# One fused attention and FFN kernel on one core: the sums move to VectorE, the job clusters are regrouped

## The reference, cut to what matters

```python
lat, ctx = layernorm(layernorm(x)), layernorm(context)
q, k, v = lat @ Wq, ctx @ Wk, ctx @ Wv                   # 16 heads of 64
attn = softmax(clip(q @ k.T * 64 ** -0.5, -11, 11))
x = x + tanh(g_xattn) * ((attn @ v) @ Wo + bo)
# FFN: weights rounded in blocks of 32 (lpbq_dequant), activations to 16 bits (act_qdq)
h = act_qdq(layernorm(x))
up, gate = act_qdq(h @ Wup.T), act_qdq(h @ Wgate.T)
gate = act_qdq(gate * fixed_qdq_u16(sigmoid(gate)))
x = x + tanh(g_ffn) * (act_qdq(gate * up) @ Wdown.T)
```

## Time and profile before

| | |
|---|---|
| median of 3 runs | 1286.16 us (1285.85 to 1286.87) |
| the profiled execution | 1289.14 us, span of its instructions 1287.2 us |
| PE busy | 1137.3 us |
| DVE busy | 1114.6 us |
| ACT busy | 599.4 us |
| POOL busy | 735.1 us |
| mean granted clock of TensorE | 0.962 of 2.4 GHz |

### The profile page before, as it was taken

One profiled execution on the slowest core, in us unless ns is written; L12 is line 12 of the kernel. 1 busy time (PEld: TensorE's weight loads), 2 busy tenths in 40 slices (PEclk: granted clock), 3 DMA queues, 4 the chain that ended last, 5 costly groups with the idle time before them and its releaser, 6 DMA issues.

```text
span 1287.2 us, 21518 instructions
## 1 busy us (share of the span) xinstructions
PE 1137.3 (88%) x8427; PEld 497.1 (39%) x8427; DVE 1114.6 (87%) x1435; ACT 599.4 (47%) x682; POOL 735.1 (57%) x457
## 2 busy tenths in 40 slices
PE   4999999999999999999999999998789987699028
PEld 2443333333333333333333333333223332487028
DVE  7588988898889888988898889899899999848986
ACT  2454444444444444444444444443345443249542
POOL 1596666666666666666666666667676565102400
PEclk9999999999999999999999999999899999699559
DMA  4000000000000000000000020000000000000002
GB/s 153 1 2 13 6 1 1 17 2 1 1 18 1 1 1 17 1 1 1 18 1 1 1 69 23 2 1 1 1 1 1 2 1 1 1 1 1 0 1 66
DMA packets 17108, 13.90 MB, mean 11 GB/s; under 512 B 2222, under 2 KB 16751, under 8 KB 17007
## 3 DMA queue, kind: packets, MB, share of 16 engines
q1 hardware_dynamic: 17006, 12.53, 3.1%
HBM read 10.43 MB, written 2.10 MB: 10 GB/s over the span
## 4 chain that ended last, share of the span: by engine, by line
PE 48%; DVE 34%; issue 11%; ACT 6%; POOL 1%; DMA 0%; POOLq 0%; SPq 0%; DVEq 0%
PE ps L938 14%; DVE e_buf L667 13%; PE ps L922 13%; PE ps L1033 6%; DVE rden L635 5%; DVE oT L643 4%; DVE acc L628 4%; PE ps L860 3%; PE ps L869 3%; PE ps L852 3%; PE ps L895 3%; ACT e_buf L446 2%; PE ps L880 1%; DVE xacc L658 1%; ACT z L501 1%
## 5 line engine op out<-in xcount | busy, mean ns | idle before, releaser
L347 POOL TENSOR_TENSOR acc<-acc,e_buf 128x512 f32<-128x512 f32 (+1 forms) x352 | 574.2, 1631 | 289.3 <-DVE e_buf L667 284.7
L446 ACT ACTIVATE e_buf<-ps 128x1024 f32<-128x1024 f32 x416 | 426.2, 1025 | 475.0 <-PE ps L922 467.6
L667 DVE TENSOR_SCALAR e_buf<-e_buf 128x1024 f32<-128x1024 f32 x416 | 475.1, 1142 | 116.7 <-ACT e_buf L446 114.3
L938 PE MATMUL ps<-e_buf,vb 64*64 64x512 f32 x3328 | 444.6, 605 | 61.1 <-DVE e_buf L667 44.8
L628 DVE TENSOR_TENSOR acc<-acc,e_buf 128x512 f32<-128x512 f32 (+1 forms) x352 | 259.8, 738 | 0.0
L938 PEld LDWEIGHTS ps<-e_buf,vb 64*64 64x64 f32 x3328 | 113.1, 133 | 294.7 <-issue 166.3
L922 PE MATMUL ps<-qb,kb_even 64*64 64x512 f32 x1664 | 216.9, 592 | 1.3 <-ACT e_buf L446 1.3
L922 PE MATMUL ps<-qb,kb_odd 64*64 64x512 f32 x1664 | 217.7, 593 | 0.0
L347 POOL TENSOR_TENSOR acc<-e_buf 128x512 f32<-128x512 f32 x32 | 81.8, 2556 | 70.3 <-DVE e_buf L667 70.3
L922 PEld LDWEIGHTS ps<-qb,kb_odd 64*64 64x64 f32 x1664 | 64.2, 134 | 116.0 <-issue 111.8
L635 DVE RECIPROCAL rden<-ps 128x128 f32<-128x128 f32 x124 | 109.0, 919 | 0.0
(11 more groups left out here) (105 smaller groups left out, 754.4 us busy)
## 6 DMA issues: line engine op xcount, KB each, us to landing
xacc<-in_x_dram SPq DMA_DIRECT2D x4, 512.0 KB, 7.5
wst<-in_L_xattn_Wkv_dram SPq DMA_DIRECT2D x16, 128.0 KB, 2.4
out_dram<-z SPq DMA_DIRECT2D x8, 256.0 KB, 2.1
e_buf<-in_ctx_dram SPq DMA_DIRECT2D x3, 512.0 KB, 4.7
wst<-in_L_xattn_Wq_dram SPq DMA_DIRECT2D x8, 128.0 KB, 2.3
wo_raw<-in_L_xattn_Wo_dram SPq DMA_DIRECT2D x8, 128.0 KB, 3.1
z<-in_L_ffn_w_gate_dram SPq DMA_DIRECT2D x1, 768.0 KB, 4.9
z<-in_L_ffn_w_up_dram SPq DMA_DIRECT2D x1, 768.0 KB, 6.8
```

What stands on the lines that cost most here:

```text
L347: pool.tensor_tensor(acc[0:r, t0 % 2, 1, :], a, e_buf[0:r, (ST * t0 + st) % E_BUFS, 1, :], ALU.add).then_inc(sum_b, 1)
L446: nc.scalar.activation(e_buf[:, g % E_BUFS, :, :], sc[:, g % 2, :, :], ACT.Exp, scale=float(DH) ** -0.5).then_inc(exp_done, 1)
L667: dve.tensor_scalar(tile, tile, EXP_LO, EXP_HI, ALU.max, ALU.min).then_inc(clip_done, 1)
L938: ins = pe.matmul(ps_o[DH * h:DH * h + DH, half, :], vb[rows, p % 2, st, DH * h:DH * h + DH], e_buf[rows, g % E_BUFS, h, :], start=(st == ...
```

## The change

The sums: each tile's both halves are added by one DVE instruction of 128x1024, and POOL keeps only the scaling of Wo in the loop. E_BUFS goes from 4 to 6. The bias is added by DVE, in segment 0. The jobs: up to segment 27, q joins k and v at step 0; y of segment t - 2 (before: of t - 1, at step 10) and den of t - 1 (before: at step 4) form a cluster at step 6. ACT takes q at step 2 and copies den to SBUF at step 8; SP spreads one row for each head over 64 partitions, DVE inverts 128x8, SP stores that to DRAM and loads it back as a broadcast; scale_out of t - 2 is at DVE's step 3 and add_y at its step 8. From segment 28 on (WT0), den is inverted as before. The weights: one piece in each second segment from 14 (WQ0) on, with both multiplies on DVE, at steps 3 to 6; their DMAs are issued in segment 4.

```diff
-WQ0, WT0 = SEGS - 7, SEGS - NBS
-E_BUFS = 4
+WQ0, WT0 = SEGS // 2 - 2, SEGS - NBS
+E_BUFS = 6
...
     if p < PAIRS:
-        jobs = [(0, ("k", p, t % NBS)), (0, ("v", p, t % NBS)), (4, ("q", t + 1)), (4, ("den", t - 1))]
-    else:
-        jobs = [(0, ("wT", wm, 0)), (0, ("wT", wm, 1)), (4, ("q", t + 1)), (4, ("den", t - 1)), (6, ("wT", wm, 2))]
+        jobs = [(0, ("k", p, t % NBS)), (0, ("v", p, t % NBS)), (0, ("q", t + 1))]
+        if t >= 2:
+            jobs += [(6, ("y", t - 2, 0)), (6, ("y", t - 2, 1))]
+        return jobs + [(6, ("den", t - 1))]
+    jobs = [(0, ("wT", wm, 0)), (0, ("wT", wm, 1)), (4, ("q", t + 1)), (4, ("den", t - 1)), (6, ("wT", wm, 2))]
+    if t == WT0:
+        jobs += [(6, ("y", t - 2, 0)), (6, ("y", t - 2, 1))]
     return jobs + [(10, ("y", t - 1, 0)), (10, ("y", t - 1, 1))]
...
+            def turn_denominator(t):
+
+                await_taken(sp, ("den", t))
+                if t:
+                    sp.wait_ge(inv_done, t)
+                for h in range(2):
+                    sp.dma_start(den_spread[DH * h:DH * h + DH, :],
+                                 den_row[DH * h:DH * h + 1, :].rearrange("a (p e) -> a p e", p=DH)).then_inc(den_landed, 16)
+                sp.wait_ge(inv_done, t + 1)
+                sp.dma_start(inv_rows.rearrange("h (p e) -> (h p) e", p=DH), inv_spread[:, :]).then_inc(inv_stored, 16)
+                sp.wait_ge(inv_stored, 16 * (t + 1))
+                for h in range(2):
+                    sp.dma_start(rden[DH * h:DH * h + DH, :],
+                                 inv_rows[h:h + 1, :].to_broadcast([DH, NB])).then_inc(inv_landed, 16)
+
             def run(seg):
...
+                if seg.t0 == NBS:
+                    load_ffn_weights()
+                if seg.t0 % NBS == NBS - 1 and (seg.t0 + 5) // NBS < PAIRS:
+                    p = (seg.t0 + 5) // NBS
+                    await_taken(sp, ("q", seg.t0), seg)
+                    sp.wait_ge(wo_scaled, p - 1)
+                    load_pair(p, p % 2)
+                if 1 <= seg.t0 < WT0:
+                    turn_denominator(seg.t0 - 1)
...
-                    pool.tensor_tensor(acc[0:r, t0 % 2, 1, :], a, e_buf[0:r, (ST * t0 + st) % E_BUFS, 1, :],
-                                       ALU.add).then_inc(sum_b, 1)
...
+            def den_take(seg, t):
+                key = ("den", t)
+                await_job(act, key, seg)
+                if t:
+                    act.wait_ge(den_landed, 32 * t)
+                nc.scalar.copy(den_row[:, :], ps_m[:, bank_of(key), :]).then_inc(job_taken[bank_of(key)], 1)
...
-                    if st == 6 and t0 + 1 < SEGS:
+                    if st == (2 if p < PAIRS else 6) and t0 + 1 < SEGS:
                         q_take(seg, t0 + 1)
+                    if st == 8 and t0 < WT0:
+                        den_take(seg, t0 - 1)
...
+            def w_multiply(w, row, ready, done):
+
+                blocks = wpiece[w].rearrange("p (n e) -> p n e", e=QB)
+                dve.wait_ge(ready, w + 1)
+                dve.tensor_tensor(blocks, blocks, wsc[:, w, row, :].unsqueeze(2).to_broadcast([P, WBLK, QB]),
+                                  ALU.mult).then_inc(done, 1)
+
+            def add_e(seg, st):
...
-                dve.tensor_tensor(acc[0:r, t0 % 2, 0, :], a, e_buf[0:r, (ST * t0 + st) % E_BUFS, 0, :],
-                                  ALU.add).then_inc(sum_a, 1)
+                dve.tensor_tensor(acc[0:r, t0 % 2, :, :], a, e_buf[0:r, (ST * t0 + st) % E_BUFS, :, :],
+                                  ALU.add).then_inc(summed, 1)
+
+            def add_bias(b):
...
+                rows = xacc[:, 4 * b:4 * b + 4, :]
+                dve.tensor_tensor(rows, rows, bo_t[:, :].unsqueeze(1).to_broadcast([P, 4, DM]), ALU.add).then_inc(bias_added, 1)
...
+            def invert_spread(t):
+
+                dve.wait_ge(den_landed, 32 * (t + 1))
+                dve.reciprocal(inv_spread[:, :], den_spread[:, :]).then_inc(inv_done, 1)
...
+                    if t0 == 0 and 4 <= st < 4 + NBS:
+                        add_bias(st - 4)
...
+                    if WT0 <= t0 < WT0 + 3:
+                        for j in {3: (0, 1), 8: (2,)}.get(st, ()):
+                            w_low(t0 - WT0, j)
+                    if st == 8 and 2 <= t0 <= WT0:
+                        add_y(seg, t0 - 2, 0)
+                        add_y(seg, t0 - 2, 1)
+                    if st == 3 and 2 <= t0 <= WT0:
+                        scale_out(seg, t0 - 2)
+                    if st == 11 and 1 <= t0 < WT0:
+                        invert_spread(t0 - 1)
+                    for c in ((), range(4))[t0 >= WT0]:
                         if st == (4 if last else 6) + c // 2:
                             invert(seg, t0 - 1, c)
...
+                    if WQ0 <= t0 < WQ0 + 12 and (t0 - WQ0) % 2 == 0:
+                        w = (t0 - WQ0) // 2
+                        if st == 3:
+                            w_scales(w)
+                        if st == 4:
+                            w_multiply(w, 2, w_inverse, w_scaled)
+                        if st == 5:
+                            w_integers(w)
+                        if st == 6:
+                            w_multiply(w, 1, w_round, w_quant)
```

More of the change, by code:

```diff
@@ L296, in _, with load_ffn_weights @@
-            for n in range(KT):
-                sp.dma_start(wpiece[4 + n], w_down[P * n:P * n + P, :]).then_inc(in_w, 16)
+            def load_ffn_weights():
+                await_taken(sp, ("lT", NBS - 1, 1))
+                for n, w in enumerate((w_gate, w_up)):
+                    sp.dma_start(zf[:, n * FT * DM:(n + 1) * FT * DM].rearrange("p (t d) -> p t d", d=DM),
+                                 w.rearrange("(t p) d -> p t d", p=P)).then_inc(in_w, 16)
+                for n in range(KT):
+                    sp.dma_start(wpiece[4 + n], w_down[P * n:P * n + P, :]).then_inc(in_w, 16)
@@ L443, in run @@
                         s0 = max((st - E_BUFS) % ST, 1)
-                        act.wait_ge(sum_a, back.count(ST - 1, s0))
-                        act.wait_ge(sum_b, back.count(ST - 1, s0))
+                        act.wait_ge(summed, back.count(ST - 1, s0))
                     nc.scalar.activation(e_buf[:, g % E_BUFS, :, :], sc[:, g % 2, :, :], ACT.Exp,
@@ L637, in invert @@
                     ins.then_inc(job_taken[bank], 1)
+            def invert_spread(t):
+                dve.wait_ge(den_landed, 32 * (t + 1))
+                dve.reciprocal(inv_spread[:, :], den_spread[:, :]).then_inc(inv_done, 1)
             def scale_out(seg, t):
-                await_taken(dve, ("den", t), seg)
+                if t < WT0 - 1:
+                    dve.wait_ge(inv_landed, 32 * (t + 1))
+                else:
+                    await_taken(dve, ("den", t), seg)
                 dve.wait_ge(o_out, Seg(t).count(1, 1))
@@ L668, in run @@
                     if st >= 2:
-                        add_a(seg, st - 1)
+                        add_e(seg, st - 1)
                     elif st == 0 and t0 >= 1:
-                        add_a(Seg(t0 - 1), ST - 1)
-                    elif st == 1 and t0 >= 1:
+                        add_e(Seg(t0 - 1), ST - 1)
+                    elif t0 >= 1:
                         join_out(seg, t0 - 1)
+                    if t0 == 0 and 4 <= st < 4 + NBS:
+                        add_bias(st - 4)
                     last = t0 == SEGS - 1
-                    for c in ((), range(4))[t0 >= 1]:
+                    if WT0 <= t0 < WT0 + 3:
+                        for j in {3: (0, 1), 8: (2,)}.get(st, ()):
+                            w_low(t0 - WT0, j)
@@ L676, in run @@
+                    if st == 8 and 2 <= t0 <= WT0:
[6 more added lines that the diff above has]
+                    for c in ((), range(4))[t0 >= WT0]:
                         if st == (4 if last else 6) + c // 2:
                             invert(seg, t0 - 1, c)
-                    if st == (6 if last else 8) and t0 >= 1:
+                    if st == (6 if last else 8) and t0 >= WT0:
@@ L690, in run @@
+                    if st == (9 if last else 12) and t0 >= WT0:
                         add_y(seg, t0 - 1, 0)
```

37 lines of the change are left out of this document (16 added, 21 removed).

## The result

The changed kernel takes 1343.35 us (median), the kernel before 1286.51 in the same comparison: ratio 1.0432, 95% interval 1.0401 to 1.0462. The change is slower; the forecast was 1327. The profiled execution took 1339.75 us with a span of 1338.0, 50.8 more than before.

A forecast was written before the change was run, and what follows sets the result against it. PE nearly bound segments 1 to 24, DVE and POOL set the pace in 25 to 27; 20 + 1.9 + 21.6 - 21.5 + 10 + 6 - 2 + 4.5 = +40.5 gave 1329.6 us, 1327 on the median, range 1298 to 1364.

The forecast's parts named there:

- Den's wait: Cluster at step 6: den, on y0's PSUM bank, waits 2.4 us until DVE's add_y at its step 8.
- Sums: DVE's loop steps: a wide 128x1024 sum takes 1.13 us, every clip 0.60, a step 1.73 against PE's 1.72.
- cheap-sum rival: DVE's wide sum takes only 0.60 us, den waits 1.2: 1272 us, faster; chance 0.07.
- Weights: Six pieces in segments 14 to 24, 3.6 us each on DVE before add_y, making den's wait 6.0: +21.6.
- Denominators: Segments 1 to 27: reciprocals leave DVE, 3.5 us each; small landings at 4.6 us leave the new way all hidden.
- rival of late denominators: Hops of 7.6 us put scale_out 1.2 us behind in some twenty segments: +25, 1352 us; chance 0.06.
- Clock: Half-clock stretches of 1.7 us extra behind the six waits of 6 us: +10; none assumed for 2.4 us waits.
- rival "at every wait": Each of the other twenty waits of 2.4 us brings a half-clock stretch, 1.7 more: +34, 1361 us; chance 0.14.
- Segments 25 to 27: They lose their weight work: 92 us against 113.5, including three den waits of 2.4: -21.5.
- The end: Last four segments: segment 28 +6, segment 29 -2, segments 30 and 31 +4.5 with DVE full of ffn_norm.

The follow-up runs named there:

- the last experiment: Den first, weight work and scale_out at step 2, plus segment 28's y jobs at steps 8 and 11, against the kernel before: 1224.51 us, ratio 0.9505.
- the three runs: The changed kernel without its one slow-state run of 2000.48 us: 1339.75, 1341.16 and 1345.53 us, median 1341.16.

## Why the prediction was right, step by step

- **Den's wait: right in place, cause and size.** Forecast 2.4 us in 26 segments; measured 2.38 in the twenty plain ones. Putting den ahead of the y jobs, off y0's bank, removed it; taking y0 1.73 earlier took 1.73 off.
- **Sums: right.** 1.13 and 0.60 by starts; no clip is contended. The cheap-sum rival is out. The rule of the Trainium skill that the prediction named ("VectorE: DVE Perf Modes", "Why `tensor_tensor` can't do 2×_2P or 4×") agrees with the trace: the wide sum took 1.13 us from start to start, the narrow one of half its size 0.60.
- **Weights: right in size, half right in place.** The forecast put all 3.6 us of a piece in front of den, a wait of 6.0. The trace has 4.41 there and two waits in front of values:

```profile
664.24 1.09 PE L981 MATMUL ps<-e_buf,vb 64*64 64x512 f32 x8 [0.42 <-DVE e_buf L698]
...
666.84 1.09 PE L981 MATMUL ps<-e_buf,vb 64*64 64x512 f32 x8 [0.65 <-DVE e_buf L698]
...
675.12 1.98 PE L923 MATMUL ps<-acc,ones 128*64 128x512 f32 x4 [4.41 <-DVE xacc L689]
```

  Per segment 4.41 - 2.38, 0.42 and 0.65, with 0.18 more for each of the two waits in front of values: 3.5. PE's own steps moved back by what those two waits cost, so den came due later.
- **Denominators: right.** Landings of the changed kernel (KB each, median us), as in the earlier trace rows:

```profile
rden<-inv_rows SPq DMA_DIRECT2D x54, 128.0 KB, 2.8
...
den_spread<-den_row SPq DMA_DIRECT2D x54, 2.0 KB, 1.8
```

  That is faster than the 4.6 assumed, and the waits list has no wait of DVE for these landings. The rival of late denominators is out.
- **Clock: the mis-sized term.** I put +10 on the six waits with weights and nothing on the others. In segments 1 to 27 the changed kernel has thirteen half-clock stretches, the kernel with den first none. Segments 1 to 24 take 737.9 us with den first; adding den's waits (17 x 2.38 + 6 x 4.41 = 66.9) makes 804.8, and the changed kernel took 826.4: 21.6 is clock (PE's busy time, 751.6 against 730.2, says the same), and another 3.5 in segments 25 to 27 (86.4 + 3 x 2.38 = 93.5 against 97.0; 86.4 is their length with den first). So 25 instead of 10. The rival "at every wait" was wrong as well: of the twenty regular waits seven were followed by such a stretch, and all six with weights. Of the 25, some 12 stand behind those seven (at 1.65 each, an estimate), for which I had nothing; the other 13, against my 10, behind the six long waits., where 2.22 us left the clock up, said too little about 2.38. The Trainium skill ("TensorE: Matmul & The Clock Gate", "HAM oscillation — how this bites in real kernels") describes a kernel that waits 3 to 5 us for its data in front of every tile and is back at the lower clock each time. Behind the waits of 4.41 us here that was so each time, behind the shorter ones of 2.38 in seven of twenty.
- **Segments 25 to 27** gained 16.5 instead of 21.5: 3.5 of clock, and the rest my count of PE's work, 86.4 rather than 84.8.
- **The end: half right.** Segment 28 lost 6.5 (forecast 6) for the reason given, as the last experiment shows. Segment 29 gained 0.3 (forecast 2) and 30 with 31 gained 0.8, where I had them lose 4.5. Part of that is the norm's own work, which I priced from the kernel before: in these two segments its twelve 128x256 scalings have 0.41 us each instead of 0.56, and three small ones of 128x4 have 0.14 instead of 0.73, some 3.6 us together. The rest is open.

By stretches the sum was 1.9 + 51.6 - 21.5 + 8.5 = +40.5; the profile has +1.7 (segment 0), +59.1, -16.5, +5.4 and about 1 around them, +50.8. The 10 that are missing are the clock's 15, less the 5 of segments 30 and 31 and small terms. No rival took place; the median of the three runs is 14 over the forecast.

What the change would have been worth without the fault: with den first, 47 under the kernel before. It needs the sums on DVE: undone, they cost 50, while alone in the old order they gain 18. So about 30 of the 47 come only from both together. The six tiles of e_buf, the new way of the denominators and the bias on DVE were not tried apart; what each is worth is open.

## What to carry to other kernels

When jobs share a few buffers by turns, look for each job at whoever empties the buffer before it, and at what that engine has queued ahead; a third job in a cluster on two banks waits for the first one's consumer. Put the job whose consumer is quick in front. An engine that needs as long for a step as the bound one (here 1.73 us against 1.72) can't make up for work put between its steps, so side work belongs where the bound engine is in its longest cluster.

## What the runs showed of the hardware that was not expected

The same wait of PE, 2.38 us in each segment, was followed by half clock (1.2 GHz) in seven of twenty and by full clock (2.4 GHz) in the others: den 1.98 and 1.08 us in the rows above. A segment with such a stretch behind a wait of 2.38 took about 1.65 us more.

Which waits are followed by half clock is not mere chance in these profiles. With weight work at step 2, where all 26 waits are 2.39, den was at half clock in segments 5, 9, 13, 17, 21 and 25, the same block of each pair of heads, 133.2 us apart (a seventh stretch began behind den of segment 2). In the changed kernel it was 2, 5, 9 and 13 as well, up to the first segment with weights, and with y0 taken earlier it was 14, 18 and 22, three of six equal waits of 2.68. Two rows of the kernel with weight work at step 2:

```profile
760.49 1.98 PE L920 MATMUL ps<-acc,ones 128*64 128x512 f32 x4 [2.39 <-DVE xacc L689]
...
893.62 1.97 PE L920 MATMUL ps<-acc,ones 128*64 128x512 f32 x4 [2.39 <-DVE xacc L689]
```

Nor does the length of the wait alone decide. In the kernel before with the sums on VectorE, 2.18 us were followed by half clock and 2.72 by full:

```profile
909.54 1.99 PE L923 MATMUL ps<-e_buf,vb 64*64 64x512 f32 x8 [2.18 <-DVE oT L635]
...
1006.73 1.09 PE L923 MATMUL ps<-e_buf,vb 64*64 64x512 f32 x8 [2.72 <-DVE oT L635]
```

What does decide stays open. The kernel whose 26 waits were all 2.39 spread over 18 us from run to run, the changed kernel's three runs over 6, and the other experiments over 2 to 4.

A multiply of 128x768 by a broadcast factor was recorded at 0.96 us on DVE, against a mean of 1.87 on GpSimd before.
